# A Mamba scan beside a feed-forward network: one more pair of du times B made by ScalarE in turned layout

## The reference, cut to what matters

```
x = x + tanh(g_xattn) * mamba(ctx, z=layernorm(x))       # batch 4, 1024 steps, 1024 channels e, 16 states n
    u     = silu(conv(in_proj(ctx)));  dt, B, C = x_proj(u)
    delta = softplus(dt_proj(dt))
    state[e,n] = state[e,n] * exp(delta[e] * A[e,n]) + (delta[e] * u[e]) * B[n]      # step by step
    y[e]  = sum over n of state[e,n] * C[n]  + D[e] * u[e];   y = y * silu(z)
x = x + tanh(g_ffn) * route_top_128_rows( attention + gated MLP )(layernorm(x))      # per batch
```

## Time and profile before

| | us |
|---|---|
| median of 3 runs (lowest to highest) | 2769.81 (2769.69 to 2774.37) |
| the profiled execution | 2772.9 |
| its span, first to last instruction | 2771.2 |
| TensorE busy | 2531.1 (91%) |
| VectorE busy | 2000.9 (72%) |
| ScalarE busy | 1619.6 (58%) |
| GpSimd busy | 1543.0 (56%) |

### The profile page before, as it was taken

The page is one execution under the profiler, slowest core; times in us unless marked ns, Lnnn a source line. Parts: engine busy times, 40 slices in busy tenths (PEclk is TensorE's granted clock), DMA queues, the critical chain, the costliest instruction groups (busy, mean ns, idle before and its releaser), DMA issues. The chain is left out here.

```text
span 2771.2 us, 38280 instructions
## 1 busy us (share of the span) xinstructions
PE 2531.1 (91%) x13528; PEld 1845.5 (67%) x13528; DVE 2000.9 (72%) x2532; ACT 1619.6 (58%) x3482; POOL 1543.0 (56%) x866
## 2 busy tenths in 40 slices
PE   8969999999999648879999999999988799999998
PEld 3346666666666417556688888888763676488853
DVE  5679999999999776469999999999987535110000
ACT  4578888888888443277787778887752215110000
POOL 1269999999999410028899889889861000000000
PEclk9989999999999859999999999999998899999999
DMA  7732252442522397863343354353328740344442
GB/s 273 247 112 79 57 156 84 126 120 69 160 60 71 148 399 259 285 192 91 122 151 118 115 175 123 101 178 126 96 68 322 275 152 24 116 150 152 152 152 99
DMA packets 252621, 412.52 MB, mean 149 GB/s; under 512 B 50832, under 2 KB 134800, under 8 KB 249872
## 3 DMA queue, kind: packets, MB, share of 16 engines
q1 hardware_dynamic: 238928, 353.98, 39.8%
q10 hardware_dynamic: 12160, 51.39, 4.6%
q0 software_dynamic: 1344, 4.72, 0.5%
HBM read 325.09 MB, written 84.94 MB: 148 GB/s over the span
## 5 line engine op out<-in xcount | busy, mean ns | idle before, releaser
L763 POOL TENSOR_TENSOR s_x<-s_hp,k_bC 128x1024 f32<-128x1024 f32 x256 | 606.0, 2367 | 108.3 <-DVE s_hp L1297 107.8
L739 POOL TENSOR_TENSOR s_x<-s_du,k_bB 128x1024 f32<-128x1024 f32 x254 | 600.9, 2373 | 39.9 <-PE s_py L888 24.8
L888 PE MATMUL s_py<-k_ident,s_x 128*128 128x128 f32 x4096 | 516.5, 274 | 5.1 <-POOL s_x L763 4.5
L888 PEld LDWEIGHTS s_py<-k_ident,s_x 128*128 128x128 f32 x4096 | 464.0, 142 | 9.9 <-POOL s_x L763 4.9
L1222 ACT ACTIVATE s_pA<-s_delta,k_negA 128x512 f32<-128x512 f32 x512 | 334.0, 682 | 168.3 <-DVE s_x L1274 162.8
L1990 PE MATMUL l_p<-l_hT,l_ring 128*128 128x256 f32 x1792 | 390.8, 381 | 2.0 <-ACT l_hT L2095 1.4
L1990 PEld LDWEIGHTS l_p<-l_hT,l_ring 128*128 128x128 f32 x1792 | 342.7, 191 | 50.0 <-ACT l_hT L2095 1.6
L1222 ACT ACTIVATE s_x<-s_delta,k_negA 128x512 f32<-128x512 f32 x512 | 340.5, 710 | 0.0
L1100 ACT ACTIVATE s_xT<-s_duT,k_BT 128x128 f32<-128x128 f32 x1024 | 336.4, 389 | 0.1
L1297 DVE TENSOR_TENSOR_SCAN s_hp<-s_x,s_pA 128x512 f32<-128x512 f32 x256 | 310.4, 1212 | 31.6 <-ACT s_x L1222 20.6
L1297 DVE TENSOR_TENSOR_SCAN s_hp<-s_x,s_carry,s_pA 128x512 f32<-128x512 f32 x256 | 324.9, 1269 | 10.0 <-PE s_pA L870 4.3
(11 more groups left out here) (237 smaller groups left out, 3682.2 us busy)
## 6 DMA issues: line engine op xcount, KB each, us to landing
k_bC<-scratch_xd SPq DMA_DIRECT2D x32, 1024.0 KB, 11.7
scratch_ug<-p_ug ACTq DMA_DIRECT2D x16, 1024.0 KB, 4.5
k_u<-scratch_ug SPq DMA_DIRECT2D x64, 256.0 KB, 3.4
k_bB<-scratch_xd SPq DMA_DIRECT2D x32, 512.0 KB, 7.9
s_gy<-scratch_ug SPq DMA_DIRECT2D x64, 256.0 KB, 4.5
s_xt<-in_x SPq DMA_DIRECT2D x64, 256.0 KB, 4.7
scratch_x<-s_xt SPq DMA_DIRECT2D x64, 256.0 KB, 3.6
r_x<-scratch_x SPq DMA_DIRECT2D x32, 512.0 KB, 10.4
```

Source lines behind the costliest of these rows:

```text
L739: pool.tensor_tensor(out=x[:, 4 * g:4 * g + n], in0=du[:, s % 2:s % 2 + 1].broadcast_to([P, n, HALF]), in1=bB[:, into:into + n], op=ALU.mu ...
L763: pool.tensor_tensor(out=x[:, 2 * i:2 * i + 2], in0=hp_of(s, i), in1=bC[:, 2 * i:2 * i + 2], op=ALU.mult).then_inc(pool_hc, 1)
L888: last = nc.tensor.matmul(py[:, a], x[:, n, a * P:(a + 1) * P], ident[:], is_transpose=True, start=False, stop=n == NS - 1 and a == HALF / ...
```

## The change

In the second scan pair 1 goes from the diagonals to ScalarE: `TURNED` becomes (1, 3, 7) there and `SCALED` (5,). In the first scan both stay. A unit of the second scan so has 24 pieces instead of 16, in the order pair 1 (0 to 7), pair 3 (8 to 15), pair 7 (16 to 23), and a list of its own: after copying du at place 6 ScalarE makes pieces 0 to 2 of the next unit, at place 7 pieces 3 to 7, then up to 11, 12, 16, 18, 20 and 24 at places 0 to 5. The first scan's list gives the same order as before. The diagonals get a tile of their own (`diagB`) instead of the end of `bB`. GpSimd makes two diagonals a chunk instead of four in the second scan.

```diff
-TURNED, SCALED = (3, 7), {0: (1, 5), SPAN: (1, 5)}
+TURNED, SCALED = {0: (3, 7), SPAN: (1, 3, 7)}, {0: (1, 5), SPAN: (5,)}
...
-PARTS = 4 * NT
-PARTS_AT = (8, 8, 10, 12, 14, 16, 16, 5)
+PARTS_AHEAD = {0: (0, 5), SPAN: (3, 8)}
+PARTS_AT = {0: (8, 8, 10, 12, 14, 16), SPAN: (11, 12, 16, 18, 20, 24)}
...
+    turned, scaled = TURNED[first], SCALED[first]
+    from_pe = tuple(sorted(turned + scaled))
+    NT = 2 * len(turned)
...
-        free = len(states_by_pool(first))
-        diagB = bB[:, free:free + ND_B].rearrange("p n (a q) -> p n a q", q=P)
+        diagB = sb("diagB", [P, ND_B, HALF // P, P])
...
-                if last_tile and scaled:
-                    make_diagonals(chunk(s) + 1, scaled[0])
+                if last_tile and 1 in scaled:
+                    make_diagonals(chunk(s) + 1, 1)
...
-                        make_states(0, 0, PARTS_AT[-1])
+                        make_states(0, 0, PARTS_AHEAD[first][1])
...
-                    if i <= DU_COPY_AT:
-                        make_states(s, PARTS_AT[i - 1], PARTS_AT[i])
+                    if i < DU_COPY_AT:
+                        make_states(s, PARTS_AT[first][i - 1] if i else PARTS_AHEAD[first][1], PARTS_AT[first][i])
                     if i == DU_COPY_AT and s + 1 < UNITS:
                         copy_du(s + 1)
+                    if i == DU_COPY_AT:
+                        make_states(s + 1, 0, PARTS_AHEAD[first][0])
                     if i > DU_COPY_AT:
-                        make_states(s + 1, PARTS_AT[i - 1] % PARTS, PARTS_AT[i])
+                        make_states(s + 1, PARTS_AHEAD[first][0], PARTS_AHEAD[first][1])
```

More of the change, by code:

```diff
@@ L75, in __init__ @@
         self.ropes = ctx.enter_context(nc.sbuf_tensor(f"c{first}_ropes", [P, SPAN, 2 * DH], F32))
-TURNED, SCALED = (3, 7), {0: (1, 5), SPAN: (1, 5)}
+TURNED, SCALED = {0: (3, 7), SPAN: (1, 3, 7)}, {0: (1, 5), SPAN: (5,)}
 def states_by_pool(first):
-    return [n for n in range(NS) if n // 2 not in TURNED + SCALED[first]]
+    return [n for n in range(NS) if n // 2 not in TURNED[first] + SCALED[first]]
 def quad_place(first, g):
@@ L98, in sb @@
             return ctx.enter_context(nc.sbuf_tensor("k_" + name, shape, F32))
-        self.bB = sb("bB", [P, max(len(states_by_pool(first)) + 2 * len(SCALED[first]) for first in SCALED), HALF])
+        self.bB = sb("bB", [P, max(len(states_by_pool(first)) for first in SCALED), HALF])
         self.bC = sb("bC", [P, NS, HALF])
@@ L359 @@
 NPAIR = NS // 2
-NT = 2 * len(TURNED)
 HP_BUFS = 3
@@ L428, in scan_stage @@
     negA, ident, tg, BT = keep.negA, keep.ident, keep.tg, keep.BT
-    scaled = SCALED[first]
-    from_pe = tuple(sorted(TURNED + scaled))
+    turned, scaled = TURNED[first], SCALED[first]
+    from_pe = tuple(sorted(turned + scaled))
+    NT = 2 * len(turned)
     NF, ND_B = 2 * len(from_pe), 2 * len(scaled)
@@ L813, in _ @@
                 times_C(s, 5)
-                if last_tile and scaled:
-                    make_diagonals(chunk(s) + 1, scaled[1])
+                if last_tile and 5 in scaled:
+                    make_diagonals(chunk(s) + 1, 5)
                 quad(s + 1, 1)
@@ L861, in make_b @@
                 for n in (2 * i, 2 * i + 1):
-                    if i in TURNED:
-                        k = 2 * TURNED.index(i) + n % 2
+                    if i in turned:
+                        k = 2 * turned.index(i) + n % 2
                         pe.wait_ge(xT_ready, NT * s + k + 1)
@@ L1098, in make_states @@
                     if s and a == 0:
-                        act.wait_ge(b_ready, b_at(s - 1, 2 * TURNED[k // 2] + k % 2))
+                        act.wait_ge(b_ready, b_at(s - 1, 2 * turned[k // 2] + k % 2))
                     last = nc.scalar.activation(xT[:, k, a * P:(a + 1) * P], duT[:, a * P:(a + 1) * P], ACT.Copy,
-                                                scale=BT[:, chunk(s) % 2, column(2 * TURNED[k // 2] + k % 2), a:a + 1])
+                                                scale=BT[:, chunk(s) % 2, column(2 * turned[k // 2] + k % 2), a:a + 1])
                     if a == 3:
```

## The result

The changed kernel takes 2812.27 us (median; 2808.89 to 2815.94) against 2770.3 us: a ratio of 1.0149, 95% interval 1.0137 to 1.0161. It is slower by 42 us. I forecast +18 us and a range up to 2803: the direction was right, and the size was outside the range.

What follows compares the result with a forecast made beforehand. TensorE, 99.5% busy in the second scan, looked like the bound, with 16 units held by VectorE and ScalarE. Terms -3.3 + 13.1 + 5.8 + 3.0 - 0.6 = +18.0 us gave a 2787.8 us median; range 2762 to 2803.

Steps and rivals of the forecast that it cites:

- T to G: VectorE, end of product of pair 0 with C (T) to gate product's start (G): forecast 4.82 us first half, 4.62 second.
- TensorE's gain: Second scan, pair 1's b by transposes instead of diagonals: 0.92 us less TensorE work a unit, 29 us over 32 units.
- the split into units paced by TensorE and by VectorE: Second scan's 30 gate-to-gate stretches: 14 where VectorE waits for TensorE (-3.3 us), 16 held by VectorE and ScalarE's feed (+13.1).
- ScalarE's other places: Added pieces at places 6, 7 and 1 of ScalarE's order and the first unit: +3.0 us, bounds 0 and 9.
- fill at place 2: Fill work on ScalarE ahead of state 7's pieces: gate's size, exponential, logarithm 3.3 us, sigmoids or copies 2.5, together +5.8.
- G to T: VectorE, gate product's start to the next end of pair 0's product with C: said to stay in the 16 VectorE-paced units.
- (a): TensorE's time comes back if ScalarE has state 7's pieces by T + 2.7: faster, 2757 or 2741 us; chance 0.13.
- (b): No change: waits for ScalarE shrink by as much as the gates lose; 2767 to 2774 us; chance 0.12.
- (c): ScalarE paces: first halves lose 1 us more each, second halves 0.3; 21 us more, 2809 us; chance 0.11.
- (d): Granted clock falls in the two stretches without fill, some 5 us each: 2798 us; chance 0.05.

Runs made afterwards that it cites:

- e2: Kernel before, with pair 1's b in the second scan from transposes without factor B, ScalarE keeping its 16 pieces: 2755.2 us, ratio 0.9948.
- e1: Changed kernel's 24 ScalarE pieces and order, but pair 1's b still from diagonals, its pieces unread: 2807.1 us, ratio 1.0138 to the kernel before.
- e7: Kernel before, with the fill's size, exponential, logarithm and sigmoid on ScalarE done on 8 of 512 columns: 2766.2 us, ratio 0.9983.
- e8: e5 with its pieces relaid, at most two at even places, the rest at odd ones: 2765.1 us, ratio 0.9982 to the kernel before; run again, 2764.0.
- e5: Changed kernel with pair 5 turned instead of pair 1, pieces relaid, same engine loads: 2776.6 us, ratio 1.0029 to the kernel before.
- e6: Changed kernel, with the fill's size, exponential, logarithm and sigmoid on ScalarE done on 8 of 512 columns: 2786.7 us, ratio 1.0060 to the kernel before.

## Why the prediction was wrong

**What held.** The mechanism, step by step: T to G, the wait of TensorE for xT inside make_b of pair 3, the loss of TensorE's gain in units it had paced (three quiet second halves in a row at 26.00 us, forecast 25.85, before 26.25), and, roughly, the split into units paced by TensorE and by VectorE. The split was too sharp: six of the 16 stretches called VectorE's had waited 0.48 to 1.07 us at the gate for TensorE before the change, and they have 4.8 of the 5.5 us that the 16 gained in e2. (The 16 also are 10 first halves and 6 second ones, not 8 and 8, which is 0.4 us of the sum.) The Trainium skill (ScalarE: Activation LUTs, Rules for kernel authors), by whose budget the prediction weighed xT 0.37 us later, did not fit this run of pieces: four took 1.26 us, as the trace of before said.

**What failed is the size of the term "ScalarE's other places"** (+3.0, bounds 0 and 9), and two things inside T to G that stood in no term of the sum: fill work at place 1, and a slower TensorE. Summed over the 30 stretches of the profiled execution, with T and G of every unit read from VectorE's timeline (units counted from 0, a stretch named by the unit that its last gate stands in):

| | units paced by TensorE (14) | by VectorE (16) |
|---|---|---|
| T to G: before | 62.9 | 62.5 |
| forecast, with fill at place 2 | 70.0 | 77.0 |
| measured | 74.3 | 82.9 |
| G to T: before | 304.7 | 355.4 |
| measured | 302.6 | 364.9 |

T to G came out at 157.2 us, 10 over the forecast's 147.0. The fill at place 2 (+5.8) is not in these 10. In units 15 and 20, with a gate's size there, xT comes at T + 4.92 and T + 4.93, 1.87 and 1.67 us later than in quiet ones, and the five sigmoids or copies cost 2.1 us: 5.6 us in all. Three things make up the 10:

- 3.8 us is fill at place 1, which I had put at nothing. In unit 5 the norm's two activations of 1.14 us stand there, and xT comes at T + 4.87 instead of T + 3.26. In units 9 and 25 the gate's size, exponential and logarithm stand there, and xT comes at T + 4.15 and T + 4.14 instead of T + 3.06. Fill need not stand at place 2 to delay the pieces; it is enough that it makes ScalarE late for place 2.
- 4.6 us is TensorE itself. From the end of the pieces to the gate it takes 1.61 to 1.63 us in the other units whose gate waits for it, but 1.97 to 2.91 us in units 2, 5, 6, 15, 18 and 20. Unit 6 is the plainest: no norm stands in it, its pieces end at T + 3.26 as forecast (T = 1423.32), and its gate comes at T + 6.17, where e1 has T + 4.88:

```profile
1425.32 1.26 ACT L1099 ACTIVATE s_xT<-s_duT,k_BT 128x128 f32<-128x128 f32 x4
```

```profile
1426.63 1.12 PE L867 MATMUL s_pA<-k_ident,s_xT 128*128 128x128 f32 x4 [1.48 <-ACT s_xT L1099]
1427.54 1.92 PE L887 MATMUL s_py<-k_ident,s_x 128*128 128x128 f32 x8
```

- 1.6 us is 0.05 to 0.06 us a unit by which the quiet ones came later than forecast (4.88 and 4.67 for 4.82 and 4.62).

G to T was forecast to fall by some 6 us in the first group and, by the term +3.0, to rise by 3 over both, 3 us shorter in all. It fell by 2.1 in the first group and rose by 9.5 in the second: 7.4 us longer. The 9.5 are ScalarE's other places at work, past the bound of 9 in one group alone. VectorE's waits in these 16 stretches rose by 4.4 us for odd pairs' dA, 1.5 us for even pairs' and 3.5 us for the gate's sigmoid: the pieces added at other places stand ahead of a sigmoid or a dA that was just in time. e7 against the kernel before shows the cover that I had taken for free: TensorE's slower pace hid most of the fill's work on ScalarE, and the chain T, pieces, gate took the cover away. I had weighed each fill operation alone, at full slack of its place, instead of summing ScalarE's work between two waits in the units that carry fill.

**The rivals.** (a) did not come true here. Its condition was that the pieces are in time; e8 meets it for pair 5, and 6 of e2's 13.7 us come back. (b) did not either: the waits for ScalarE did not shrink by what the gates lost, they grew. (c), ScalarE as the pace, was the nearest in time (2809). As a matter of load it falls, since e5 and e8 carry the same load at 2777 and 2765; but the 9.5 us between the gates are a loss of its kind. (d), the clock, has a share, and not only in the units without fill where I had put it. In 1395 to 1403 us of the changed kernel the granted clock was 0.76, after TensorE had idled 2.39 us at xT; the same adds of pair 7 take 1.91 us there and 1.04 in e1 at full clock. The rows of the changed kernel come first, then those of e1:

```profile
1395.00:1403.00 8.00, 4.29 (x24) 3.47 (x23) 3.92 (x5) 7.66 (x20) 4.10 (x3) 0.76 0.01 2
```

```profile
1399.56 1.91 PE L887 MATMUL s_py<-k_ident,s_x 128*128 128x128 f32 x8
```

```profile
1397.00:1405.00 8.00, 4.94 (x44) 4.50 (x42) 5.02 (x5) 7.54 (x20) 5.61 (x3) 1.00 0.00 0
```

```profile
1401.25 1.04 PE L890 MATMUL s_py<-k_ident,s_x 128*128 128x128 f32 x8
```

The stretches of the other five units have 0.83 (1312 to 1320 us), 0.79 (1424 to 1432), 0.85 (1670 to 1678), 0.81 (1756 to 1764) and 0.93 (1813 to 1820). Over the six units T to G is 4.6 us longer in the changed kernel than in e1, whose ScalarE order is the same and whose gates there come 1.62 or 1.63 us after the pieces. These are the 4.6 us from above. They are about the 4 to 5 us that the changed kernel takes over e1; that the clock makes all of it is read from these windows, and no run isolates it. The six do not differ from the rest by the idle time alone: units 17, 19 and 22 also waited 1.48 or 1.49 us for xT, and their adds took 1.04 us.

## What to carry to other kernels

Work moved to an engine with idle time cost by its place in that engine's order here, not by its sum: find the instruction whose consumer is due first, and add up all that stands between the last wait and it, fill work included. The same trade was worth +42, +8 or -6 us here by which pair was moved and where its pieces were laid. When the pacing engine is relieved, look for the work that its pace had been hiding, and price that in every unit, not in the quiet one.

## What the runs showed of the hardware

The granted clock of TensorE fell to 0.76 to 0.93 in six stretches of 7 to 8 us of the changed kernel, at the level of 1.2 GHz for part of them. Just before, TensorE had waited 1.47 to 2.42 us between float32 transposes, and the next eight adds took 1.39 to 1.92 us instead of 1.04. Waits of the same 1.48 us left the adds at 1.04 us in other units, and in e6 the same wait of 2.39 us in unit 5 did too, so no rule comes out of these rows. e1 shows the other direction in its unit 5. After 3.39 us of idle time its granted clock was 0.53 from 1390 to 1397 us, while TensorE worked 6.29 of 7 us, the products with diagonals first (3.78 us for sixteen records, against 1.95 in the earlier trace rows):

```profile
1390.00:1397.00 7.00, 6.29 (x31) 6.29 (x32) 6.46 (x6) 7.00 (x13) 4.69 (x2) 0.53 0.00 1
```

From 1397 to 1405 us it was 1.00, with 2.12 us of waiting for xT in that stretch. I had not expected idle times as short as these to matter.
